# Third attention: probabilities normalised before the value product, V as the stationary operand

## The reference, cut to what matters

```python
q = (x @ Wq).reshape(B, N, 8, 64).transpose(0, 2, 1, 3)
k = (context @ Wk).reshape(B, M, 8, 64).transpose(0, 2, 1, 3)
v = (context @ Wv).reshape(B, M, 8, 64).transpose(0, 2, 1, 3)
attn = softmax(einsum('bhnd,bhmd->bhnm', q, k) * 64 ** -0.5, axis=-1)
out = einsum('bhnm,bhmd->bhnd', attn, v)
return out.transpose(0, 2, 1, 3).reshape(B, N, 512) @ Wo + bo      # added to x
```

## Time and profile before

| | us |
|---|---|
| median of 3 runs | 1812.54 |
| lowest, highest | 1801.36, 1815.06 |
| the profiled execution | 1814.79 |
| its span | 1813.0 |
| TensorE busy over the span (matmul) | 1407.7 |
| VectorE, ScalarE, GpSimd busy | 1086.5, 826.2, 545.6 |
| mean granted TensorE clock | 0.837 of full |

### The profile page before, as it was taken

The page is one execution under the profiler, slowest core; times in us unless marked ns, Lnnn a source line. Parts: engine busy times, 40 slices in busy tenths (PEclk is TensorE's granted clock), DMA queues, the critical chain, the costliest instruction groups (busy, mean ns, idle before and its releaser), DMA issues. The chain is left out here.

```text
span 1813.0 us, 44016 instructions
## 1 busy us (share of the span) xinstructions
PE 1407.7 (78%) x14972; PEld 1090.2 (60%) x14972; DVE 1086.5 (60%) x3255; ACT 826.2 (46%) x2117; POOL 545.6 (30%) x994
## 2 busy tenths in 40 slices
PE   6999979984799984089986999953298747586875
PEld 3677645552577764079985888842277635464654
DVE  4788748896888877234445666466011147766543
ACT  1666636664566654222223455510033357564543
POOL 4455411111211006700008444037400088312211
PEclk9999975686899985589997999965599966687778
DMA  4332300000000001157752111001266511010001
GB/s 142 123 117 104 115 9 2 3 3 2 23 21 20 23 22 39 52 170 204 205 164 58 41 40 38 18 26 48 87 194 192 153 45 37 11 39 10 1 1 47
DMA packets 111128, 120.12 MB, mean 66 GB/s; under 512 B 12656, under 2 KB 88432, under 8 KB 110832
## 3 DMA queue, kind: packets, MB, share of 16 engines
q1 hardware_dynamic: 83184, 91.67, 16.8%
q0 software_dynamic: 8192, 16.79, 3.3%
q10 hardware_dynamic: 19584, 9.44, 1.8%
HBM read 81.16 MB, written 36.70 MB: 65 GB/s over the span
## 5 line engine op out<-in xcount | busy, mean ns | idle before, releaser
L2245 PE MATMUL e_H<-e_xT,e_w_up 128*128 128x256 f32 x736 | 174.6, 385 | 0.0
L2091 DVE COPY e_xT<-e_pX 128x256 f32<-128x256 f32 x72 | 30.6, 425 | 215.5 <-PE e_pX L2234 215.5
L2245 PEld LDWEIGHTS e_H<-e_xT,e_w_up 128*128 128x128 f32 x736 | 137.0, 194 | 16.3
L2255 PE MATMUL e_pY<-e_w_down,e_h 128*128 128x128 f32 x992 | 124.6, 277 | 15.4 <-ACT e_h L2167 14.5
L2255 PEld LDWEIGHTS e_pY<-e_w_down,e_h 128*128 128x128 f32 x992 | 119.5, 192 | 27.1 <-issue 19.3
L2156 ACT ACTIVATE e_silu<-e_H 128x256 f32<-128x256 f32 x120 | 42.5, 382 | 163.8 <-DVE e_y L2111 89.7
L2287 POOL DMA_INDIRECT slots_in<-R,r_put x96 | 92.2, 960 | 40.0 <-issue 28.4
L2234 PE MATMUL e_pX<-W,e_rows 128*128 128x128 f32 x144 | 28.6, 281 | 95.0 <-DMA e_rows<-slots_in 93.7
L477 ACT ACTIVATE a_PT<-a_ST 128x1024 f32<-128x1024 f32 x64 | 65.5, 1024 | 79.0 <-PE a_ST L544 79.0
L432 DVE TENSOR_REDUCE a_mx<-a_S 128x8 f32<-128x1024 f32 x64 | 78.1, 1221 | 34.1 <-PE a_S L517 33.9
L2167 ACT ACTIVATE e_h<-e_H,e_w_down 128x256 f32<-128x256 f32 x128 | 50.1, 474 | 85.4 <-DMA e_w_down<-in_f_dram 55.5
(11 more groups left out here) (414 smaller groups left out, 4068.8 us busy)
## 6 DMA issues: line engine op xcount, KB each, us to landing
slots_in<-Y SPq DMA_DIRECT2D x32, 512.0 KB, 2.9
e_w_up<-in_f_dram SPq DMA_DIRECT2D x40, 384.0 KB, 3.2
e_w_down<-in_f_dram SPq DMA_DIRECT2D x32, 322.0 KB, 3.2
e_rows<-slots_in SPq DMA_DIRECT2D x72, 128.0 KB, 2.8
slots_out<-e_y ACTq DMA_DIRECT2D x72, 128.0 KB, 2.9
e_w_up<-in_f_dram SPq DMA_DIRECT2D x32, 256.0 KB, 3.4
e_w_down<-in_f_dram SPq DMA_DIRECT2D x40, 192.0 KB, 3.1
a_cK<-in_ctxT_dram SPq DMA_DIRECT2D x64, 64.0 KB, 1.9
```

Source lines behind the costliest of these rows:

```text
L2245: i = nc.tensor.matmul(H[:, banks * p + b, CHUNK * c:CHUNK * (c + 1)], up[:, p, at:at + P], xT[:, p, :], start=True, stop=True)
L2255: i = nc.tensor.matmul(pY[:, D * s:D * s + D], h[:, p, c, P * s:P * s + P], down[:, p, D * c:D * (c + 1)], start=(c == 0), stop=(c == HC - 1))
```

## The change

The probabilities are normalised before they are used. `normalise` moves up the pipeline from lag 10 to lag 8: VectorE sums the exponentials of each row in SBUF, takes the reciprocal and multiplies `Pr` in place. In `product_v` the operands change places: V (128 keys of two heads x 128 channels of the two heads, without the column of ones) is stationary, and 64 columns of `PT` stream. The result has channels on partitions and tokens along the row, which is the layout `output` needs, so `transpose_z`, `zn` and its semaphores go. ScalarE copies `pZ` straight to `zT`. `Pr` has three buffers for two, `pZ` two banks of its own (where `pO` was), `pT` is no longer shared. transpose_p and values move from lag 8 to 9, product_v from 9 to 10.

```diff
-        V = sb("V", [P, 2, 2, 4, 2, 65])
-        Pr = sb("Pr", [P, 2, 512])
+        V = sb("V", [P, 2, 2, 4, 2, 64])
+        Pr = sb("Pr", [P, 3, 512])
...
-        rden = sb("rden", [P, 2, 2, 4, 1])
-        zn = sb("zn", [P, 2, 512])
+        sums, rden = sb("sums", [P, 2, 8]), sb("rden", [P, 2, 8, 1])
...
-        pZ = pT
-        pO = ps("pO", [P, 2, 512])
+        pZ = ps("pZ", [P, 2, 512])
...
             nc.gpsimd.memset(V[:, :, :, :, :, :], 0.0).then_inc(s_ones, 1)
-            for h in range(2):
-                pool.wait_ge(s_ones, h + 1)
-                nc.gpsimd.memset(V[64 * h:64 * h + 64, :, :, :, h, 64:65], 1.0).then_inc(s_ones, 1)
-            pool.wait_ge(s_ones, 3)
...
-                free(dve, s_pt, u)
+                free(dve, s_pt, u, bufs=3)
...
             def normalise(u, p):
-                o = pO[:, :, 0:260].rearrange("p a (h c) -> p a h c", c=65)
-                done(dve, s_o, u)
-                nc.vector.reciprocal(rden[:, p], o[:, :, :, 64:65]).then_inc(s_rd, 1)
+                probs = Pr[:, u % 3, :].rearrange("p (h k) -> p h k", k=T)
+                done(dve, s_exp, u)
+                nc.vector.tensor_reduce(sums[:, p], probs, AX, ALU.add).then_inc(s_sum, 1)
+                done(dve, s_sum, u)
+                nc.vector.reciprocal(rden[:, p, :, 0], sums[:, p]).then_inc(s_rd, 1)
                 done(dve, s_rd, u)
-                free(dve, s_zt, u)
-                nc.vector.tensor_tensor(zn[:, p, :].rearrange("p (a h c) -> p a h c", a=2, c=64),
-                                        o[:, :, :, 0:64], rden[:, p].broadcast_to([P, 2, 4, 64]),
-                                        ALU.mult).then_inc(s_zn, 1)
+                nc.vector.tensor_tensor(probs, probs, rden[:, p].broadcast_to([P, 8, T]), ALU.mult
+                                        ).then_inc(s_pn, 1)
...
-            pipeline(dve, NT, [(10, normalise), (7, softmax), (5, take_k),
+            pipeline(dve, NT, [(8, normalise), (7, softmax), (5, take_k),
...
-            pipeline(act, NT, [(8, take_pt), (7, exps), (3, take_xt), (10, take_zt), (8, take_v),
+            pipeline(act, NT, [(9, take_pt), (7, exps), (3, take_xt), (10, take_zt), (9, take_v),
                                (4, take_q)], straight=True)
...
-        turnsT = Bank(NT, {"pt": (8, s_pts, 1, 1), "zt": (10, s_zts, 1, 1)})
-        turnsV = Bank(NT, {"y": (11, s_x, 1, 1), "v": (8, s_vs, 1, 1)})
+        turnsV = Bank(NT, {"y": (11, s_x, 1, 1), "v": (9, s_vs, 1, 1)})
...
             def transpose_p(u, p):
-                done(pe, s_exp, u)
-                turnsT.take(pe, "pt", u)
+                done(pe, s_pn, u)
+                free(pe, s_pts, u, bufs=1)
...
             def product_v(u, p):
                 done(pe, s_pts, u)
                 done(pe, s_vs, u)
-                free(pe, s_zn, u, bufs=1)
+                free(pe, s_zts, u)
                 for j in range(4):
                     for b in range(2):
-                        r = slice(64 * b, 64 * b + 64)
-                        i = nc.tensor.matmul(pO[r, j // 2, 130 * (j % 2):130 * (j % 2) + 130],
-                                             PT[:, p, j, r], V[:, p, b, j].rearrange("p h c -> p (h c)"),
-                                             start=True, stop=True)
-                i.then_inc(s_o, 1)
-
-            def transpose_z(u, p):
-                done(pe, s_zn, u)
-                turnsT.take(pe, "zt", u)
-                for j in range(4):
-                    i = nc.tensor.transpose(pZ[:, P * j:P * j + P], zn[:, p, P * j:P * j + P], w("ident"))
+                        at = P * j + 64 * b
+                        i = nc.tensor.matmul(pZ[:, p, at:at + 64], V[:, p, b, j].rearrange("p h c -> p (h c)"),
+                                             PT[:, p, j, 64 * b:64 * b + 64], start=True, stop=True)
                 i.then_inc(s_zt, 1)
...
-            pipeline(pe, NT, [(8, transpose_p), (11, output), (9, product_v), (10, transpose_z),
-                              (8, values), (6, scores), (3, transpose_x), (4, project)], straight=True)
+            pipeline(pe, NT, [(9, transpose_p), (11, output), (10, product_v),
+                              (9, values), (6, scores), (3, transpose_x), (4, project)], straight=True)
```

More of the change, by code:

```diff
@@ L1111, in attention2_stage @@
         s_v, s_vs, s_S, s_mx, s_sub, s_exp = [sem(n) for n in ("v", "v_out", "scores", "max", "sub", "exp")]
-        s_pt, s_pts, s_o, s_rd, s_zn = [sem(n) for n in ("pt", "pt_out", "o", "rden", "zn")]
+        s_pt, s_pts, s_sum, s_rd, s_pn = [sem(n) for n in ("pt", "pt_out", "sums", "rden", "p_normalised")]
         s_zt, s_zts, s_y, s_x = [sem(n) for n in ("zt", "zt_out", "y", "x")]
@@ L1154, in softmax @@
                 top = mx[:, p, :].rearrange("p (j h) -> p h j", h=2)
-                out = Pr[:, p, :].rearrange("p (j h k) -> p h j k", h=2, k=T)
+                out = Pr[:, u % 3, :].rearrange("p (j h k) -> p h j k", h=2, k=T)
                 done(dve, s_S, u)
@@ L1185, in _ @@
         def _(act):
-            act.wait_ge(s_ones, 3)
+            act.wait_ge(s_ones, 1)
             def take_xt(u, p):
@@ L1200, in take_v @@
                 done(act, s_v, u)
-                free(act, s_o, u)
+                free(act, s_zt, u)
                 for h in range(2):
@@ L1209, in exps @@
                 done(act, s_sub, u)
-                nc.scalar.activation(Pr[:, p, :], Pr[:, p, :], ACT.Exp, scale=SCALE).then_inc(s_exp, 1)
+                nc.scalar.activation(Pr[:, u % 3, :], Pr[:, u % 3, :], ACT.Exp, scale=SCALE).then_inc(s_exp, 1)
             def take_pt(u, p):
                 done(act, s_pt, u)
-                free(act, s_o, u)
+                free(act, s_zt, u)
                 nc.scalar.activation(PT[:, p].rearrange("p j t -> p (j t)"), pT[:, :], ACT.Copy
@@ L1220, in take_zt @@
                 free(act, s_y, u)
-                nc.scalar.activation(zT[:, p].rearrange("p j t -> p (j t)"), pZ[:, :], ACT.Copy
+                nc.scalar.activation(zT[:, p].rearrange("p j t -> p (j t)"), pZ[:, p], ACT.Copy
                                      ).then_inc(s_zts, 1)
-            pipeline(act, NT, [(8, take_pt), (7, exps), (3, take_xt), (10, take_zt), (8, take_v),
+            pipeline(act, NT, [(9, take_pt), (7, exps), (3, take_xt), (10, take_zt), (9, take_v),
                                (4, take_q)], straight=True)
         turnsQ = Bank(NT, {"xt": (3, s_xts, 1, 1), "q": (4, s_qs, 1, 1)})
-        turnsT = Bank(NT, {"pt": (8, s_pts, 1, 1), "zt": (10, s_zts, 1, 1)})
-        turnsV = Bank(NT, {"y": (11, s_x, 1, 1), "v": (8, s_vs, 1, 1)})
+        turnsV = Bank(NT, {"y": (11, s_x, 1, 1), "v": (9, s_vs, 1, 1)})
         @block.tensor
@@ L1276, in transpose_p @@
             def transpose_p(u, p):
-                done(pe, s_exp, u)
-                turnsT.take(pe, "pt", u)
+                done(pe, s_pn, u)
+                free(pe, s_pts, u, bufs=1)
                 for j in range(4):
-                    i = nc.tensor.transpose(pT[:, P * j:P * j + P], Pr[:, p, P * j:P * j + P], w("ident"))
+                    i = nc.tensor.transpose(pT[:, P * j:P * j + P], Pr[:, u % 3, P * j:P * j + P], w("ident"))
                 i.then_inc(s_pt, 1)
```

## The result

| | before | changed |
|---|---|---|
| median, us | 1812.51 | 1875.6 |
| lowest, highest | 1801.36, 1815.06 | 1868.51, 1882.03 |
| span of the profiled execution | 1813.0 | 1866.6 |
| one round of the third attention, median of the 24 from the 8th to the last transpose of x | 6.69 | 8.50 |

The ratio is 1.0352, with a 95% interval of 1.03 to 1.0404: 63 us slower, well outside the range of 1803 to 1840 us. The product with V cost what was forecast, or a little less. The time went into a wait that no step and no rival of the prediction had.

What follows compares the result with a forecast made beforehand. The prediction took TensorE's list in the third attention as the bound. Its terms, 5.7 + 3.7 + 0.3 - 0.6 = +9.1 us, gave 1821 us (+0.5%) on the footing of the median, range 1803 to 1840 us.

Steps and rivals of the forecast that it cites:

- The product with V: On TensorE, 16 records paced by weight loads plus start and shape switch: 1.93 us against 1.04 before, bounds 1.80 to 2.15.
- What bounds the kernel: Third attention: only TensorE is at its limit, busy 140.00 of 140 us; its list takes 6.69 us a round.
- The failed step: SyncE's queue: V's context tile is released a round later, but the queue runs rounds ahead; cost nothing in mid-stage.
- All three: Rivals: weight load hides, 1794 us, 10%; load and stream don't overlap, 1849 us, 13%; VectorE becomes bound, 1848 us, 3%.
- The step on weight loads: TensorE's product: loading 128 f32 weight columns, not the short stream, spaces records, 0.112 us each, bounds 0.107 to 0.129.
- the start of 0.05 behind its waits: TensorE's product: an added 0.05 us for starting behind its waits, within the 1.93 us.
- The round without the wait: TensorE's round in the third attention grows by 0.21 us, 0.08 to 0.43, to 6.90 us.
- The shape switch: TensorE: a change of tile shape between groups of matmuls costs 0.09 us.
- VectorE: Sum about 0.6 us and multiplication 0.69, 0.6 more a round, hidden by the 1.31 us wait before the maximum; cost 0.
- Start and end: Ends of the third attention: start -0.6 and +0.3 us; from last scores to last residual's end 22.7 against 19.0, +3.7.
- The sum: Whole kernel: 5.7 for 27 rounds, +3.7 end, +0.3 and -0.6 start, +9.1 us together; bounds +5 to +17.

Runs made afterwards that it cites:

- a1: The changed kernel with SyncE's load of the context tile for V at lag 4, not 3: 1814.82 us, ratio 1.0023 to the kernel before.
- a2: The kernel before, without the change, with SyncE's load of the context tile for V at lag 2, not 3: 1870.38 us, ratio 1.0328.
- a3: On top of a1, each matmul of the product with V streams 8 of its 64 columns: 1817.35 us in one execution.
- a4: On top of a1, each matmul of the product with V loads only 64 weight columns, the second head left out: 1785.22 us in one execution.
- b1: On top of a1, V's zero blocks left out, 64*64 matmuls in two diagonal quarters of the array: 1799.41 us, ratio 0.9896 to the kernel before.
- b3: On top of a1, GpSimd's bias addition waits for the reciprocal, to run beside VectorE's multiplication of P: median round 7.00 us; no kernel time given.
- b2: On top of b1, scores stand ahead of values in TensorE's list: 1794.0 us, ratio 0.988 to the kernel before.

## Why the prediction was wrong, point by point

- **What bounds the kernel** was right for the kernel before: a1, with TensorE busy throughout, follows TensorE's list to 0.1 us.
- **The failed step** is this sentence: "The context tile for V is released a round later on SyncE's queue, which runs rounds ahead." The first half is the cause of the whole loss. The second half was never looked up. SyncE doesn't run rounds ahead. It stands behind values in every round, issuing V's load and, right behind it, K's; in the kernel before K's load was one round ahead of its reader, 7.0 us for a transfer of about 1.9. "Taking P and V a round later costs nothing in mid-stage: each consumer moves with them" held for consumers on the engines and overlooked the producer of the input, whose free slot is signalled by the moved step, and what is queued behind that producer's wait. In numbers, the lead of 7.0 us fell by a round (6.7) to 0.3, and TensorE had to wait out the rest of the 1.9. a1 and a2 show it from both sides.
- **No rival had it.** All three were about durations on TensorE or VectorE. A wait that takes the place of the work removed was not among them, although lags were changed on VectorE, ScalarE and TensorE and not on SyncE.
- **The product**: forecast 1.93 (bounds 1.80 and 2.15), measured 1.82 and 1.83. The step on weight loads, on which the sum rested, is right, and a3 and a4 show it in isolation. The Trainium skill's advice for 64 moving columns ("TensorEngine Tiling (Array Packing)", Performance Considerations), to swap the operands and tile the columns twofold, speaks for the layout before. This case agrees: that layout, with 64 columns stationary, was the cheaper one, 1.04 us against 1.83. A record took 0.109 and not 0.112, and the start of 0.05 behind its waits didn't come. The round without the wait grew by 0.09 us, at the low end of 0.08 to 0.43.
- **The shape switch** of 0.09 us is right: output went from 1.03 to 0.93 (a1).
- **VectorE**: the sum takes 0.68 and not 0.6, the multiplication 0.69 or, beside GpSimd, 1.05. Hidden, as forecast; the wait before the maximum is 1.09 us in the changed kernel and 1.40 in a1, forecast 1.3.
- **Start and end**, read in a1: from the last scores to the last residual's end 22.3 us, forecast 22.7 against 19.0 before. The head of the stage, from its first memset to the 8th transpose of x, is 1.2 us shorter (44.7 to 43.5) where -0.6 + 0.3 stood. It was charged too much.
- **The sum** without the wait: +9.1 forecast. In the stage of a1 it is +4.6 (246.7 against 242.1), in its ratio +4. The term that was mis-sized is the round, 0.21 for 0.09 over 27 rounds.

## What to carry to other kernels

When a step moves by a round in a hand-written pipeline, list for each tile that it reads who refills it, and what stands behind that refill in the issuing queue. A refill that waits for the moved step can hold back a load for quite another step. Measure the lead of each load, from its issue to its reader, against its time to land; "hidden" is a number of us, and moving the reader of its neighbour by a round takes a round away. And on TensorE, with f32 and short streams, count weight columns before streamed ones; a block-diagonal stationary operand pays for its zeros (1.83 us with them, 1.08 without).

## What the runs showed of the hardware

- A record with 128 f32 weight columns takes 0.11 us at full clock whether 8 or 64 columns stream (a3, a1); one with 64 weight and 64 streamed columns takes about half of that (a4).
- Two 64*64 matmuls in diagonal quarters, each with a PSUM bank of its own, run together: 32 records in 1.08 us (b1).
- VectorE with two SBUF operands and GpSimd's addition stretch when they overlap, 0.47 to 0.90 us for GpSimd alone when it starts 0.11 us into the multiplication (b3), 0.69 to 0.97 and 0.47 to 0.68 for both when it starts 0.60 us into it (b2). At 0.67 to 0.70 us (changed kernel) both stretch in 15 of 20 rounds, to 1.05 and 0.68, and neither in 5.
- Behind a wait of 2.46 us TensorE's granted clock fell to 0.50 for part of a round (changed kernel, 1049 to 1052 us); in a2 it fell four times. Waits of 1.4 to 1.6 us mostly passed without a fall, and one of 2.59 us did too.
